# A time recurrence of 512 steps: one operation of VectorE placed forward, a wait more on GpSimd, and GpSimd's loop written out

## The reference

```python
def _derivative(q, p, drive, coupling, bias):
    i_couple = jnp.tanh(q) @ coupling.T
    dq = q - q ** 3 / 3.0 - p + drive + i_couple + bias
    dp = EPSILON * (q + ALPHA - BETA * p)
    return (dq, dp)

def _rk4_step(q, p, drive, coupling, bias):
    dq1, dp1 = _derivative(q, p, drive, coupling, bias)
    dq2, dp2 = _derivative(q + 0.5 * DT * dq1, p + 0.5 * DT * dp1, drive, coupling, bias)
    dq3, dp3 = _derivative(q + 0.5 * DT * dq2, p + 0.5 * DT * dp2, drive, coupling, bias)
    dq4, dp4 = _derivative(q + DT * dq3, p + DT * dp3, drive, coupling, bias)
    q_next = q + DT / 6.0 * (dq1 + 2 * dq2 + 2 * dq3 + dq4)
    p_next = p + DT / 6.0 * (dp1 + 2 * dp2 + 2 * dp3 + dp4)
    q_next = jnp.clip(q_next, -CLAMP, CLAMP)
    p_next = jnp.clip(p_next, -CLAMP, CLAMP)
    return (q_next, p_next)
...
(_, _), q_trace_tbn = jax.lax.scan(scan_fn, (q0, p0), drive_tbn)
...
x = x + _L0_attn_ref(_L0_cond_ref(cond_2048, cond_2048, x, coupling, bias), Wqkv_w, Wqkv_b)
x = x + _L0_ffn_ref(_L0_cond2_ref(x, cond_2048, ...), ...)
```

## Time and profile before

| | us |
|---|---|
| median of 3 runs | 5410.8 |
| lowest and highest run | 5400.78, 5411.15 |
| the profiled execution | 5413.09 |
| its span, first to last instruction | 5411.5 |

### The profile page before, as it was taken

One profiled execution on the slowest core, in us unless ns is written; L12 is line 12 of the kernel. 1 busy time (PEld: TensorE's weight loads), 2 busy tenths in 40 slices (PEclk: granted clock), 3 DMA queues, 4 the chain that ended last, 5 costly groups with the idle time before them and its releaser, 6 DMA issues. The chain is left out here.

```text
span 5411.5 us, 212004 instructions
## 1 busy us (share of the span) xinstructions
PE 4425.1 (82%) x78665; PEld 3826.1 (71%) x78665; DVE 4190.9 (77%) x25454; ACT 2313.5 (43%) x10538; POOL 1674.5 (31%) x5965
## 2 busy tenths in 40 slices
PE   6977777777777777777776878699999999879899
PEld 5966666666666666666665666587777787668777
DVE  8999999999999999999995667677777777631123
ACT  3343333333333333333333656555555555432243
POOL 2444444444444444444443222223332222100000
PEclk5555555555555555555556999799999999989999
DMA  2000000000000000000002010222222222141121
GB/s 95 27 1 1 1 1 1 1 1 1 1 1 1 1 1 1 1 1 1 1 1 80 9 44 17 87 75 67 86 86 78 82 75 68 34 148 39 52 90 39
DMA packets 147685, 188.32 MB, mean 35 GB/s; under 512 B 9148, under 2 KB 79364, under 8 KB 147112
## 3 DMA queue, kind: packets, MB, share of 16 engines
q1 hardware_dynamic: 145712, 182.66, 10.2%
q0 software_dynamic: 624, 0.75, 0.1%
q10 hardware_dynamic: 904, 0.15, 0.0%
HBM read 143.66 MB, written 39.90 MB: 34 GB/s over the span
## 5 line engine op out<-in xcount | busy, mean ns | idle before, releaser
L249 PE MATMUL bank<-tanh_parts,w_lo 128*128 128x4 f16 x32768 | 1208.4, 169 | 679.3 <-ACT tanh_parts L189 679.3
L249 PEld LDWEIGHTS bank<-tanh_parts,w_lo 128*128 128x128 f16 x32768 | 1035.4, 105 | 855.2 <-ACT tanh_parts L189 853.9
L189 ACT ACTIVATE tanh_parts<-ys 128x8 f16<-128x8 f32 x4096 | 861.6, 210 | 1760.4 <-DVE ys L347 1760.4
L257 PE MATMUL bank<-tanh_parts,w_hi 128*128 128x8 f16 x32768 | 1212.6, 173 | 2.0 <-issue 2.0
L257 PEld LDWEIGHTS bank<-tanh_parts,w_hi 128*128 128x128 f16 x32768 | 1066.4, 104 | 7.7 <-issue 2.1
L347 DVE TENSOR_TENSOR_SCAN ys<-mix,bank 128x24 f32<-128x24 f32 x4096 | 820.8, 202 | 105.7 <-PE bank L257 2.2
L190 ACT ACTIVATE tanh_full<-ys 128x8 f32<-128x8 f32 x4096 | 805.0, 197 | 0.0
L337 DVE TENSOR_TENSOR tanh_parts<-tanh_full,tanh_parts 128x8 f16<-128x8 f32 x4096 | 679.5, 166 | 1.6 <-ACT tanh_full L190 1.6
L1246 POOL TENSOR_TENSOR t_w_qk<-t_raw_qk,t_w_qk 128x512 fp32r<-128x512 f32 x128 | 168.0, 1334 | 710.1 <-ACT t_w_qk L1410 710.1
L515 PE MATMUL t_bank<-t_x,t_w_qk 128*128 128x512 f32 x1536 | 360.9, 391 | 12.8 <-DVE t_x L1666 12.8
L515 PEld LDWEIGHTS t_bank<-t_x,t_w_qk 128*128 128x128 f32 x1536 | 289.6, 189 | 73.8 <-DVE t_x L1666 13.5
(11 more groups left out here) (232 smaller groups left out, 9143.4 us busy)
## 6 DMA issues: line engine op xcount, KB each, us to landing
t_raw_qk<-L_cond_qkv_w_dram SPq DMA_DIRECT2D x128, 256.0 KB, 3.3
t_raw_vo<-L_cond_qkv_w_dram SPq DMA_DIRECT2D x16, 1024.0 KB, 5.2
t_raw_vo<-L_cond_out_w_dram SPq DMA_DIRECT2D x16, 1024.0 KB, 5.2
n<-t_parts SPq DMA_DIRECT2D x14, 1024.0 KB, 6.6
g_raw<-L_cond_ffn_w_dram SPq DMA_DIRECT2D x8, 1024.0 KB, 10.1
g_x<-n SPq DMA_DIRECT2D x8, 1024.0 KB, 11.8
xT<-L_cond_ada_w_dram SPq DMA_DIRECT2D x8, 768.0 KB, 5.4
t_x<-n SPq DMA_DIRECT2D x6, 1024.0 KB, 7.0
```

Of the source, the lines that this page charges most:

```text
L189: act.activation(tanh_parts[:, u, at, :, 0], ys[:, s, at, :, 2], ACT.Tanh, scale=1.0 / SCALE).then_inc(s_th, 1)
L249: pe.matmul(sums[:, :, 2], w_lo[:, w_of, k, m * P:(m + 1) * P], tanh_parts[:, u, k, :, 0], start=(m % 2 == 0 and k == 0), stop=False, skip ...
L257: last = pe.matmul(sums[:, :, 1:3], w_hi[:, w_of, k, m * P:(m + 1) * P], tanh_parts[:, u, k], start=False, stop=(m % 2 == 1 and k == C - 1 ...
```

## The change

Three edits in `scan_phase`.

1. In `stage_3` of VectorE, the second `low_part(t, 3, 1)` stands directly behind the first and ahead of `sloped`, where it stood behind `sloped`.
2. In GpSimd's `one_step`, before `gq<-q`, a wait for `s_rate` at `t * 3 + 1` is added: VectorE's `rate` of stage 0 must be finished.
3. GpSimd's loop of 128 rounds of four steps becomes 512 steps written out, with the step as a constant in addresses and waits. The register arithmetic and the clear of `s_pool` go.

```diff
--- before.py
+++ after.py
@@ -29,7 +29,6 @@
 
 DT, EPSILON, ALPHA, BETA, CLAMP = 0.01, 0.08, 0.7, 0.8, 20.0
 STAGES = 4
-UNROLL = 4
 PE_UNROLL = 2
 HALVES = (slice(0, C // 2), slice(C // 2, C))
 
@@ -424,8 +423,8 @@
                 own("rate_3", stt(rate[:, 3], ps_[:, 3], -BETA, y3))
                 cubed(y3, GAIN[3])
                 low_part(t, 3, 0)
+                low_part(t, 3, 1)
                 sloped(y3, THIRD + GAIN[3])
-                low_part(t, 3, 1)
                 v.wait_ge(s_psum, t + 1)
                 own("moved", stt(p_new[:, :, :], rate[:, 3], EPSILON * H / 3, p_sum[:, :, :]))
                 after("slope")
@@ -469,16 +468,17 @@
 
                 g.wait_ge(s_pool, mark)
 
-            def one_step(t, at):
-                g.tensor_copy(drive_now[:, :, :], drive[:, :, :, bass.ds(at, 1)].rearrange("p c b o -> p c (b o)")).then_inc(s_now, 1)
+            def one_step(t):
+                g.tensor_copy(drive_now[:, :, :], drive[:, :, :, t]).then_inc(s_now, 1)
                 g.wait_ge(s_now, t + 1)
                 g.wait_ge(s_p, t + 1)
                 tt(net[:, :, :], drive_now[:, :, :], p[:, :, :], ALU.subtract).then_inc(s_net, 1)
                 g.wait_ge(s_clip, t + 1)
+                g.wait_ge(s_rate, t * 3 + 1)
                 own(tt(gq[:, 0], q[:, :, :], by_rest, ALU.mult))
                 g.wait_ge(s_net, t + 1)
                 of_net = own(tt(gq[:, 1], net[:, :, :], by_third_h, ALU.mult))
-                g.tensor_copy(trace[:, :, :, bass.ds(at, 1)].rearrange("p c b o -> p c (b o)"), q[:, :, :])
+                g.tensor_copy(trace[:, :, :, t], q[:, :, :])
                 after(of_net)
                 tt(thirds[:, 0], gq[:, 0], gq[:, 1], ALU.add).then_inc(s_third, 1)
                 g.wait_ge(s_rate, t * 3 + 2)
@@ -492,10 +492,8 @@
                 after(both)
                 tt(p_sum[:, :, :], gp[:, 3], p[:, :, :], ALU.add).then_inc(s_psum, 1)
 
-            with g.Fori(0, T // UNROLL) as steps:
-                g.sem_clear(s_pool)
-                for i in range(UNROLL):
-                    one_step(steps * UNROLL + i, steps * UNROLL + i)
+            for t in range(T):
+                one_step(t)
             g.wait_ge(s_clip, T + 1)
             g.tensor_copy(trace[:, :, :, T], q[:, :, :]).then_inc(s_trace, 1)
```

## The result

| | us |
|---|---|
| changed kernel, median | 5378.3 (5376.7 to 5379.2) |
| kernel before, beside it | 5411.0 (5400.8 to 5412.4) |
| ratio | 0.9943, 95% interval 0.9926 to 0.9961 |
| predicted | 5352 (5336 to 5380) |

The kernel is faster, by 33 us where 59 were forecast. The range held the time, by 2 us; the size of the gain was wrong by nearly half.

A forecast was written before the change was run, and what follows sets the result against it. The prediction took the recurrence step of 5.55 us, set by what ends last in each stage, as the bound. Gains of 0.065 (stage 3) and 0.05 (stage 0) made 0.115 us a step, x 512 = 59 us: 5352 us, range 5336 to 5380.

The forecast's parts named there:

- What bounds the kernel: Recurrence steps of 5.55 us, a little over half the span, set by what ends last in each stage.
- The ring: Each stage's cycle: VectorE scan, ScalarE tanh twice, TensorE's low and high products, then the next stage's scan.
- the undisturbed pair: Stage 1: high-product weight loads run 0.50 us without a gap; the scan starts 0.42 us after they start.
- the two stages that differ: Stage 3: loads 0.60 us, scan 0.52 after, from a late second low_part; stage 0: scan at 5.10, not 5.04, from mix.
- Part 1: Swap in stage 3: an earlier second low_part removes TensorE's gap, gaining 0.08 us in three steps, 0.02 in the fourth, mean 0.065.
- What is late next: Stage 3 after the swap: pushed-back slope, then mix, hold the scan to 3.61, 0.08 us earlier than 3.69.
- Part 2, the gain: Stage 0: with GpSimd waiting for the rate, mix ends at 4.95 instead of 5.00, gaining 0.05 us a step.
- Part 2, the cost: Moved GpSimd operations stand beside stage 0's scans and early stage 1; taken as nothing, one hit priced at 0.04 us.
- rival of one hit: GpSimd lengthens one VectorE operation in stage 1, leaving 0.075 us a step, 38 us: 5372; chance 0.14.
- Part 3: GpSimd's loop written out: taken as 0, between -0.01 and the price of slow code loading.
- the wait does nothing: Stage 0's mix stays at 0.22 and its scan at 5.10; only 33 us gained: 5378; chance 0.08.
- Code loading: 50 more GpSimd instruction packets each stall 1.6 us, 80 us: 5432; chance 0.03 shared with three hits.

The follow-up runs named there:

- e5: The kernel before with only the new GpSimd wait for the rate added, loop of four and stage 3 kept: 5387.7 us beside 5407.3, ratio 0.9961.
- f1: The changed kernel with GpSimd's two waits before gq<-q in reverse order, rate first: 5360.3 us, ratio 0.9898; timed again, 5365.1 us, ratio 0.9915.
- e2: The kernel before with the low_part swap of stage 3 and the new GpSimd wait, loop of four kept: 5356.1 us, ratio 0.9898.
- e8: The changed kernel without the new GpSimd wait and with GpSimd's copy of q to trace moved to stage 2: 5370.1 us, ratio 0.9917.
- e4: The changed kernel with VectorE's p_stages<-rate,p moved from between stage 0's scans to behind stage 1's second low_part: 5432.9 us, ratio 1.0039.
- e7: The changed kernel with GpSimd waiting for the end of stage 0's first scan instead of the rate: 5368.5 us, ratio 0.9916.
- e1: The kernel before with only the low_part swap of stage 3, GpSimd untouched: 5380.0 us, ratio 0.9942.
- g1: f1 with stage 3's cub ahead of rate and slope between the two low_parts: 5371.5 us, ratio 0.9931, beside f1's 5365.1.

## Why the prediction was right and wrong

*What bounds the kernel*: right. The ring of each stage, the undisturbed pair of 0.50 and 0.42, and the two stages that differ from it are what the trace after shows, and the whole change of the time lies there.

*Part 1*: right. The scan of stage 3 was to come 0.44 after the weight loads and does; the gain was to be 0.08 in three steps and 0.02 in the fourth, mean 0.065, and is 0.069 and 0.009, mean 0.054. "What is late next", `slope` and `mix`, was the right limit.

*Part 2, the gain*: right. `rate` 0.17, `mix` 0.18, the scan 0.44 after L256 (0.43 forecast), 0.045 us in place of 0.05, and by e5 worth 20 us alone. `gq<-q` started 0.14 after `rate`, the 0.15 of the rows of `p` and `net`, and `thirds` was in time.

*Part 2, the cost*: this is the step that failed, a term put at nothing. "The cost of part 2 is where the three operations go: from 4.98 to 5.72 they stand beside both scans of stage 0 and the first operations of stage 1 ... I take nothing for it." Between those two scans stands a third operation, `p_stages<-rate,p`, with two inputs from SBUF. The reason given was `slope` of stage 0, which kept its 0.17 beside `gq<-net`. It is a weak one: `slope` starts 3 ns ahead of `gq<-net`, and it was GpSimd's operation that lost there, 0.250 against 0.221 in the changed kernel. The rival of one hit spoke of `cub` and the second `low_part` of stage 1, not of this one. The numbers to see it were there: `gq<-net` at 4.98 + 0.18 = 5.16 and `p_stages` 0.12 after a scan at 5.05 (5.10, then 5.22, before), so at 5.17, nearly the same moment. The price was at hand too, 0.06. It came to 0.068 on that operation (0.217 against 0.149) and, after the slack behind it, 0.032 a step or 16 us, and f1, where the hit is gone, is faster by 0.034 a step. With it, 59 less 16 is 43; the rest, 8 us, is the 0.016 by which the two gains were rated too high (0.115 against 0.099). So a step takes 5.484 us and not 5.43 to 5.44.

*Part 3*: "I take 0" was right for the code itself: f1, with the same written-out loop, takes the same 5.450 us a step as e2 with the loop kept. It was wrong in that writing out the loop decides which of two waits rides on the instruction, and so the moment at which `gq<-net` starts. The prediction took the 0.15 of an operation with two waits, which for `gq<-q` is the written-out case, and did not ask what it would meet.

*The rivals*: "the wait does nothing" gives 5378, the time measured, by a mechanism that did not happen: that the two agree is chance, and only the trace tells them apart. The forecast's own band (5343 to 5362) missed; the whole range held the time only by the room it gave to this rival and to "one hit". "One hit" (5372) was the true kind, in the wrong place. Code loading was nothing, and the rule of the page "Runtime: NRT & Kernel Launch" of the Trainium skill, section "Instruction fetch mechanics", that straight code is fetched ahead, agrees with the trace here: 51 more packets and no idle on "issue". The rule of "GPSIMD Engine Reference", section 1, of the same skill, that the two engines contend where VectorE has two inputs in SBUF, fits every operation that was hit, and no scan was; but many overlaps cost nothing, and the distance of the starts tells more.

## What to carry to other kernels

Where two engines work in a fixed rhythm, a change that moves the work of one must be laid against every operation of the other at its new place, also against the small one between two large ones; overlap shares do not tell which are hit, starts to within 0.1 us tell more. Of several waits on an instruction, the one that ends last starts it earlier if the instruction carries it itself: here it had to stand first in the code, and that was worth 0.065 us on GpSimd. GpSimd was not what ended last, so this alone is worth nothing; the 17 us came because it took `gq<-net` away from `p_stages`, and elsewhere an earlier start could as well make a hit. A gain that is visible in one stage and absent in the total has gone into another stage: compare the lengths of all stages first.

## What the runs showed of the hardware

An operation of VectorE with two inputs in SBUF, of 16 numbers on each partition, can get longer when it starts soon after the start of a GpSimd operation. These are the clearest pairs of the kernels above, as means over the steps of one trace, in ns. The last column is the same operation where no GpSimd operation starts within 0.12 us ahead of it:

| starts after GpSimd's by | operation (GpSimd's) | length | undisturbed |
|---|---|---|---|
| 3 | mix (copy to trace), before | 222 | 182, changed kernel |
| 13 | cub (copy of drive_now), before | 229 | 170, fourth step before |
| 19 | known (gp), e8 | 226 | 162, e4 |
| 23 | rate (p_sum), e8 | 230 | 173, stages 1 and 2 |
| 31 | p_stages (gq<-net), changed kernel | 217 | 149, before |
| 39 | known (gq<-q), e7 | 208 | 149, before |
| 61 | p_new (copy of drive_now), e2 | 192 | 168, before |
| 75 | known (gp), e1 | 176 | 162, e4 |
| 82 | rate (gq<-net), before | 196 | 168, changed kernel |
| 93 | p_stages (gq<-net), f1 | 153 | 149, before |
| 96 | mix of stage 3 (copy of drive_now), fourth step before | 192 | 174, other steps |

So the price falls from 40 to 70 ns for starts within 40 ns to 4 to 30 ns for starts 60 to 100 ns behind, and there it is not the same for all. If both start within about 0.02, it can be GpSimd's operation that loses instead: in g1 `rate` starts 13 ns behind the copy of `drive_now` and takes 169 in 320 steps, with the copy at 251, and 230 in 120 steps, with the copy at 204; in e5's fourth step `p_new` starts 18 ns behind the copy and keeps 169, with the copy at 254. An operation that starts ahead of GpSimd's was not longer (`slope` of stage 0 at 168, 3 ns ahead of `gq<-net`, before). The scans, with one input in PSUM, were at no distance longer than 205 ns in any of these kernels, alone or not. What arbitrates between the two is not shown by these runs.

On GpSimd, a wait that is an instruction of its own and ends last delays what stands behind it by 0.065 us more than a wait on the instruction itself (`gq<-q` 0.145 in the changed kernel against 0.080 in f1 after the end of `rate`).
